# The second FFN product of a gated cross-attention block: one fp32 product per chunk against three split ones, from the thirteenth tile on

## The reference, cut to what matters

```python
x = x + jnp.tanh(g_xattn[0]) * xattn(layernorm(x), ctx, ctx, ...)
xf = layernorm(x)
expert_weights, expert_indices = top_k(softmax(xf @ w_router.T), 2)
h = silu(einsum('td,edh->eth', xf, w1)) * einsum('td,edh->eth', xf, w3)
y = einsum('eth,ehd->etd', h, w2)          # E 8, H 352, D 256
x = x + jnp.tanh(g_ffn[0]) * sum over the 2 chosen experts of weight * y
```

## Time and profile before

| what | us |
|---|---|
| median of three runs | 851.28 (850.83 to 853.52) |
| the profiled execution, its own time | 846.11 |
| its span, first to last instruction | 844.4 |
| TensorE busy | 805.9 (95%) |
| mean granted TensorE clock, share of full | 0.986 |
| one FFN tile, from one A to the next | 4.21 |
| start of the first FFN product A | 559.1 |

### The profile page before, as it was taken

One profiled execution on the slowest core, in us unless ns is written; L12 is line 12 of the kernel. 1 busy time (PEld: TensorE's weight loads), 2 busy tenths in 40 slices (PEclk: granted clock), 3 DMA queues, 4 the chain that ended last, 5 costly groups with the idle time before them and its releaser, 6 DMA issues.

```text
span 844.4 us, 22220 instructions
## 1 busy us (share of the span) xinstructions
PE 805.9 (95%) x7529; PEld 698.5 (83%) x7529; DVE 489.9 (58%) x1170; ACT 441.4 (52%) x1120; POOL 525.0 (62%) x599
## 2 busy tenths in 40 slices
PE   7889999999999999999999999889999999999994
PEld 6789998999999999999999998767777777777773
DVE  5566777877777777777777777634622222222221
ACT  3356676676676677677666766555222222222221
POOL 6555565476667657666665765346677765656652
PEclk8989999999999999999999999999999999999998
DMA  5867777786676666676557566764443444434432
GB/s 158 191 150 174 197 185 192 180 205 156 171 176 158 169 165 158 153 178 154 136 147 175 139 156 138 213 146 79 57 60 62 75 64 64 64 62 65 64 57 30
DMA packets 99845, 112.33 MB, mean 133 GB/s; under 512 B 29276, under 2 KB 81124, under 8 KB 99736
## 3 DMA queue, kind: packets, MB, share of 16 engines
q1 hardware_dynamic: 79720, 92.48, 44.2%
q0 software_dynamic: 18512, 17.60, 13.5%
q10 hardware_dynamic: 1504, 0.85, 0.4%
HBM read 35.48 MB, written 17.53 MB: 63 GB/s over the span
## 4 chain that ended last, share of the span: by engine, by line
PE 78%; DVE 14%; issue 3%; DMA 2%; SPq 1%; ACT 1%; POOL 1%; ACTq 0%; POOLq 0%; DVEq 0%
PE ps L1474 18%; PE ps L1535 10%; PE ps L1198 9%; PE ps L1215 9%; PE ps L1229 7%; DVE negmax L922 7%; PE ps L1183 7%; PE ps L1330 3%; PE ps L1389 3%; PE ps L1222 3%; PE ps L1493 2%; PE ps L1418 2%; PE ps L1322 1%; DVE xa L907 1%; PE ps L1304 1%
## 5 line engine op out<-in xcount | busy, mean ns | idle before, releaser
L922 DVE TENSOR_REDUCE negmax<-ps 112x2 f32<-112x750 f32 x256 | 239.8, 938 | 110.4 <-PE ps L1215 109.2
L623 ACT ACTIVATE probs<-ps 125x448 f32<-125x448 f32 x384 | 209.6, 547 | 67.6 <-PE ps L1183 63.1
L402 POOL DMA_DIRECT2D stack<-negmax_t x128 | 68.0, 535 | 164.3 <-ACT negmax_t L678 153.1
L1183 PE MATMUL ps<-stack 97*125 97x224 f32 x768 | 166.5, 299 | 2.6 <-DMA stack<-negmax_t 1.8
L1215 PE MATMUL ps<-stack 96*112 96x376 f32 x512 | 140.5, 356 | 12.6 <-DVE negmax L922 11.8
L526 POOL DMA_INDIRECT out_dram<-y,idx x63 | 100.8, 1600 | 70.0 <-issue 30.9
L1183 PEld LDWEIGHTS ps<-stack 97*125 97x125 f32 x768 | 125.3, 189 | 9.3 <-DMA stack<-negmax_t 1.9
L722 ACT ACTIVATE silu<-ps 128x352 f32<-128x352 f32 x63 | 29.3, 465 | 184.4 <-PE ps L1474 184.4
L1134 DVE TENSOR_TENSOR h<-silu,ps 128x352 f32<-128x352 f32 x63 | 32.8, 521 | 147.3 <-PE ps L1474 147.2
L1535 PE MATMUL ps<-w_sb,h_t 128*128 x378 | 92.3, 380 | 0.7 <-ACT h_t L728 0.7
L1215 PEld LDWEIGHTS ps<-stack 96*112 96x112 f32 x512 | 71.5, 177 | 22.9 <-DVE negmax L922 19.8
(11 more groups left out here) (239 smaller groups left out, 1514.3 us busy)
## 6 DMA issues: line engine op xcount, KB each, us to landing
stack<-split SPq DMA_DIRECT2D x252, 150.0 KB, 2.9
stack<-split SPq DMA_DIRECT2D x127, 94.0 KB, 2.6
ctx_raw<-in_ctx_dram SPq DMA_DIRECT2D x29, 375.0 KB, 3.8
stack<-split SPq DMA_DIRECT2D x127, 56.0 KB, 2.8
out_dram<-xa SPq DMA_DIRECT2D x32, 112.0 KB, 2.5
xn_scratch<-xn SPq DMA_DIRECT2D x32, 112.0 KB, 2.2
xa<-in_x_dram SPq DMA_DIRECT2D x7, 448.0 KB, 4.2
w_sb<-in_L_ffn_w_dram SPq DMA_DIRECT2D x16, 176.0 KB, 2.8
```

The lines of the kernel that those rows point to most:

```text
L402: gp.dma_start(dst[:, :, SKP + SQ * h:SKP + SQ * h + SQ], negmax_t[4 * h:4 * h + 4, half, :].bitcast(f32)).then_inc(s_nmrow[half][c % NSLO ...
L623: act.activation(probs[:, n % NP, :], ps[0:KW, EXPB + k % 2, 0:4 * SQ], ACT.Exp).then_inc(s_exp, 1)
L922: dve.tensor_reduce(negmax[:, half, :, p4], ps[0:SQ, m1:m2 + 1, 0:SK], axis=AX.X, op=ALU.max, negate=True).then_inc(s_max, 1)
L1183: last = pe.matmul(ps[0:KW, EXPB + k % 2, QW * m:QW * m + QW], stack[:, place_of(b), p, KW * ch:KW * ch + KW], stack[:, place_of(b), p, SK ...
```

## The change

From tile 13 on (`PARTS`) Y is the sum of three products of fp32r operands in place of one of fp32: `ht_h w2_h + ht_h w2_l + ht_l w2_h`. `ht_h` is the turned h copied from PSUM and rounded by ScalarE, `ht_l` the difference of the two, made by VectorE at the start of iteration t+1 ahead of h of t+1; TensorE waits for it (`s_htl`) ahead of all of Y. The same three products of w2: the rounded parts `w2_h` are made by ScalarE, two copies in each of the iterations 4 to 11, the rests `w2_l` by VectorE, two subtractions in each of the iterations 5 to 12. `ctx_l`, `ctx_h`, `ctx_raw` and `probs` move into the space that is given back before the FFN's tensors are made, so that w2_h and w2_l have room.

```diff
-        ctx_l, ctx_h = sb("ctx_l", ...), sb("ctx_h", ...)
-        probs = sb("probs", [KW, NP, 4 * SQ])
-        ctx_raw = sb("ctx_raw", [P, DC, SK])
+        ctx_l, ctx_h = (late.enter_context(nc.sbuf_tensor(n, [P, NSLOT, DC, SKP], f32r)) for n in ("ctx_l", "ctx_h"))
+        ctx_raw = late.enter_context(nc.sbuf_tensor("ctx_raw", [P, DC, SK], f32))
+        probs = late.enter_context(nc.sbuf_tensor("probs", [KW, NP, 4 * SQ], f32))
         late.close()
...
+        ht_h, ht_l = (sb(n, [P, FC, P], f32r) for n in ("ht_h", "ht_l"))
+        w2_h, w2_l = (sb(n, [P, FC, NE, EMB], f32r) for n in ("w2_h", "w2_l"))
...
+        SPLIT, PARTS = 4, 13
...
+        def w2_parts(e):
+            n = F - P * (FC - 1)
+            return [tuple(w[:, 0:FC - 1, e, :] for w in (w2_sb, w2_h, w2_l)), tuple(w[0:n, FC - 1, e, :] for w in (w2_sb, w2_h, w2_l))]
...
# ScalarE, iteration t, between silu and turned(t + 1)
-                    act.activation(h_t[:, :, :], ps[:, HTB, 0:FC * P], ACT.Copy).then_inc(s_h_t, 1)
+                    if t - 1 < PARTS:
+                        act.activation(h_t[:, :, :], ps[:, HTB, 0:FC * P], ACT.Copy).then_inc(s_h_t, 1)
+                    else:
+                        act.activation(ht_h[:, :, :], ps[:, HTB, 0:FC * P].rearrange("p (c q) -> p c q", c=FC), ACT.Copy).then_inc(s_h_t, 1)
+                if 0 <= t - SPLIT < NE:
+                    if t == SPLIT:
+                        act.wait_ge(s_pv, 4 * B)
+                        act.wait_ge(s_w2, 16 * (NE + FC - 1))
+                    for raw, high, low in w2_parts(t - SPLIT):
+                        act.activation(high, raw, ACT.Copy).then_inc(s_w2h, 1)
...
# VectorE, iteration t, ahead of h of t
+                if t - 1 >= PARTS:
+                    dve.wait_ge(s_h_t, t)
+                    dve.tensor_tensor(ht_l[:, :, :], ps[:, HTB, 0:FC * P].rearrange("p (c q) -> p c q", c=FC), ht_h[:, :, :].bitcast(f32),
+                                      ALU.subtract).then_inc(s_htl, 1)
...
# VectorE, at the end of iteration t
+                if 0 <= t - SPLIT - 1 < NE:
+                    for n, (raw, high, low) in enumerate(w2_parts(t - SPLIT - 1)):
+                        dve.wait_ge(s_w2h, 2 * (t - SPLIT - 1) + n + 1)
+                        dve.tensor_tensor(low, raw, high.bitcast(f32), ALU.subtract).then_inc(s_w2l, 1)
...
# TensorE, ahead of turning h
                     wait(pe, s_h_t, o)
+                    wait(pe, s_htl, o - PARTS)
...
# TensorE, Y of tile o = t - 1
                     pe.wait_ge(s_h_t, o + 1)
                     wait(pe, s_y, o)
-                    for c in range(FC):
-                        n = min(P, F - P * c)
-                        last = pe.matmul(ps[:, YB, 0:EMB], h_t[0:n, c, :], w2_sb[0:n, c, bass.ds(e_o, 1), :].rearrange("p e d -> p (e d)"),
-                                         start=(c == 0), stop=(c == FC - 1))
+                    if o == PARTS:
+                        pe.wait_ge(s_w2l, 2 * NE)
+                    wait(pe, s_htl, o - PARTS + 1)
+                    terms = ((h_t, w2_sb),) if o < PARTS else ((ht_h, w2_h), (ht_h, w2_l), (ht_l, w2_h))
+                    for j, (ht, w) in enumerate(terms):
+                        for c in range(FC):
+                            n = min(P, F - P * c)
+                            last = pe.matmul(ps[:, YB, 0:EMB], ht[0:n, c, :], w[0:n, c, bass.ds(e_o, 1), :].rearrange("p e d -> p (e d)"),
+                                             start=(j + c == 0), stop=(j == len(terms) - 1 and c == FC - 1))
```

More of the change, by code:

```diff
@@ L69, in flamingo @@
         half2, lnv2, lnr2, lnt2 = (sb(n, [SQ, 1]) for n in ("half2", "lnv2", "lnr2", "lnt2"))
-        ctx_l, ctx_h = sb("ctx_l", [P, NSLOT, DC, SKP], f32r), sb("ctx_h", [P, NSLOT, DC, SKP], f32r)
         xn, xn_t = sb("xn", [SQ, EMB]), sb("xn_t", [P, DC, SQ])
@@ L134, in flamingo @@
         s_x = [sem(f"s_xload{n}") for n in range(4)]
+        s_w2h, s_w2l, s_htl = sem("s_w2h"), sem("s_w2l"), sem("s_htl")
         s_chi, s_clo, s_whi, s_wlo = (sem(n) for n in ("s_chi", "s_clo", "s_whi", "s_wlo"))
```

## The result

The changed kernel takes 874.74 us (median of 4, 872.85 to 877.31) against 851.06 (850.52 to 853.52): 1.028 times, 95% interval 1.0251 to 1.031, 23.7 us slower. The profiled execution took 872.85, its span 871.1, which is 26.7 over the span of before. Tiles are counted from 0: tile 13 is the fourteenth.)

What follows compares the result with a forecast made beforehand. TensorE bounds the kernel now; after the change its sequencer's path sets a 4.57 us tile against 4.21. 17.6 us over 49 gaps, 0.4 for splitting w2 and 0.5 at the end give 18.5: 870 us, range 856 to 891.

Steps and rivals of the forecast that it cites:

- main case: TensorE's sequencer, waiting for ht_l then issuing Y, delays the next A: tile 4.57 us against 4.21; chance 0.52.
- Y's issue: TensorE's sequencer issuing Y's nine products, three of them cheap and six with address: 0.66 us, lowest sensible 0.53.
- The array: Y's nine one-record products on TensorE: 1.10 us in place of 1.30, a gain of 0.20 per tile.
- The extra wait: Ahead of Y, the wait for ht_l needs its own instruction: 0.15 us with the semaphore, 0.11 less if carried.
- second rival: Y begins late but the sequencer isn't the limit: +0.05 us a tile, 854.7 us in all; chance 0.08.
- Splitting w2: ScalarE and VectorE work in iterations 4 to 12: hidden except where VectorE is full, +0.4 us once.
- The end: After the last Y, with no A following: it starts 0.65 us later and is 0.2 shorter, +0.5 us.
- The array decides: Wait for ht_l and Y's issue stay hidden: tile 4.01 us, 842 us in all, faster; chance 0.08.
- Only Y's start slips: Y begins late, nine products issue in below 0.35 us: +0.05 us a tile, 854.7 us; chance 0.08.
- Every product forms its address: Issue of Y's nine products takes 1.0 to 1.17 us: +0.70 to +0.87 a tile, 887 to 895; chance 0.28.
- The clock: TensorE's clock falls because it idles 0.5 us in each tile: 924 us or more; chance 0.02.
- Two records again: Y's new form runs as two records a product: +0.9 us in Y for 49 tiles, 895 us; chance 0.02.

Runs made afterwards that it cites:

- e3: Changed kernel with only the three products ht_h times w2_h, the wait for ht_l kept: 850.91 us, 1.0062 times the kernel before.
- e4: Changed kernel with the next tile's expert number loaded ahead of Y's waits, nothing left out: 849.57 us, 1.0043 times the kernel before.
- e5: Changed kernel with the wait for ht_l moved behind Y's first six products, nothing left out: 840.64 us, 0.9861 times the kernel before.
- e2: Changed kernel without h's subtraction and the wait for ht_l, the last three products using ht_h instead: 838.0 us, 0.9893 times the kernel before.
- e6: Changed kernel with both the early expert load and the wait for ht_l behind six products: 841.34 us, 0.9877 times the kernel before.
- e1: Changed kernel with Y left in fp32 from h_t, subtraction and wait ahead of Y kept: 859.47 us, 1.0162 times the kernel before.
- e7: Changed kernel with w2 split and tensors moved, but Y in fp32 in all tiles: 850.15 us, 0.9987 times the kernel before.
- e8: Kernel before with only the early load of the next expert number added: 851.06 us, 1.0005 times the kernel before.

## Why the prediction was right

The forecast was 870 in a range of 856 to 891 and 0.87 for slower; 874.74 came. The main case named the place (between Y's issue and the next A), the reason (the sequencer, in order, behind the wait for ht_l), and three address forms. The sum was 5 us low. That this is the cause, and not only the number, is what e3, e4 and e5 show: less work on the array doesn't help, and moving one load or one wait does.

**The steps.** Predicted, then the mean of the same distances over the steady tiles of the changed kernel, worked out from starts and ends in the trace:

| step of a tile, us | predicted | measured |
|---|---|---|
| end of ht_h to ht_l's start | 0.03 | 0.03 |
| the subtraction | 0.55 | 0.56 |
| end of ht_l to Y's first address | 0.15 | 0.15 |
| Y's issue, first address to expert load | 0.66 | 0.74 |
| expert load to A's address | 0.75 | 0.78 |
| A's address to A's weight load | 0.10 | 0.10 |
| from there to the next end of ht_h | 2.33 | 2.33 |
| tile | 4.57 | 4.69 |

**Y's issue was the mis-sized term.** I had taken 0.10 for a product with the 46 ns form, 0.09 with the 32 ns form and 0.03 without an address, on the ground that one record less is issued. In the trace after, the address starts of a tile at its best are 0.124 apart in the first form, exactly as for the two-record products of before, and 0.113 in the second; the three products without an address add nothing, since the expert load starts 0.113 behind the last address. That is 0.71, and single tiles go to 0.88, so the mean is 0.74. The number of records doesn't matter for this queue, the number of address instructions does. 0.08 of the missing 0.12 a tile is this, 0.03 the expert load, which takes 0.75 to 0.92 from tile to tile where I took the 0.75 of one tile. The gaps were miscounted too: an A follows the Y of tiles 13 to 60 only, 48 gaps and not 49. They came to 22.9 us, 0.477 each, where the sum had 49 x 0.36 = 17.6. The longer tile is 48 x 0.117 = 5.6 of the difference, and the gap too many takes 0.4 back.

**The array.** 1.10 for nine products was forecast from value_proj; e2 shows 1.07. The Trainium skill ("TensorE: Matmul & The Clock Gate", Back-to-back issue gap) would give 0.98, an estimate from its isolated gap of 0.109; e2 is nearer to the row. What the change could have earned is 0.22 a tile; e6 earns it (mean 3.995 against 4.213), e5 0.19.

**The extra wait.** 0.11 for a wait instruction of its own was right. In e1 the late start of Y costs 0.25 by itself; the prediction had the same step in its second rival (+0.05 with nine products), and e4's 4.26 is that rival, met once the load is out of the way.

**Splitting w2.** Predicted 0.4 us once, from VectorE being full in tiles 7 and 8. The place is right, the size isn't: the turns of h that were to wait are 0.45 in the chain where 0.33 is usual.

```profile
612.90 0.45 PE ps L1519 x3
```

0.12 us; in e7 the same turns are 0.50, 0.17 more than usual, which its median can't show. h ahead of them had moved by 1.1 and not by the forecast 1.7 (612.24 against 608.21, with this execution 2.91 later there), in part because the two subtractions of a tile take 1.02 together and not 1.1. **The end** came out 0.75 longer, silu of the last tile to the end of the span 16.0 against 15.3, where 0.5 was forecast.

**The rivals.** The array decides: fell (e3 has 0.9 us less array work and isn't faster). Only Y's start slips: this is what e1 and e4 show, and in e4 it is some 15% of the changed kernel's loss (0.0043 of 0.028). Every product forms its address: six do, not nine. The clock: 1.00 in the window above and in every other one from 570 to 820 us; it read 0.83 from 560 to 570, ahead of any split product. Two records again: one record each.

**Slips in the working.** The main case was said to span 860 to 878, but its own bounds give 858 to 877. The rival with two records a product put nine of them at 2 us; at the 0.217 of a record in the earlier trace rows eighteen would take 3.9. Neither changes the argument.

The Trainium skill ("Perfetto Trace Analysis", Sequencer-only Instruction) has the next instruction fetched only after one of the sequencer's own is done. The table agrees: the expert load never starts ahead of Y's last address, and e4 and e8 show what the order alone is worth.

## What to carry to other kernels

Before a wait is added to an engine's stream, list what stands behind it in that queue though it doesn't need it: here an expert load and an address, 0.9 us of the sequencer's work, and the wait turned a gain of over 1% into a loss of 3%. Put the wait at the first instruction that reads the data, and move loads into registers ahead of it. A product whose address comes from a register costs the queue the same whether it is one record or two, so a split into more products is paid in addresses; the three products that used w2_h a second time formed none and added nothing.

## What the runs showed that I had not expected

A busy share of 97% for TensorE, where the prediction looked for some 90%, in a stretch where the array idles for about 0.7 us in each tile of 4.7; the chain's "issue" and a first record of A that is 0.1 us longer tell it. And the spread: before, every tile from the seventh on was 4.21 us, in the changed kernel 4.63 to 4.86. The sequencer's own jitter, above all in the expert load (0.75 to 0.92), had been there all along behind the 0.5 us of lead; e6 has it hidden again, with every gap after tile 14 at 3.99 to 4.00.
